# Twice the rows fetched by ScalarE, and another order for the last tiles of a graph layer

## The reference

```
h   = relu(layernorm(x))                        # x: 12500 nodes x 128
xp  = h @ lin1
C   = 0.5 * (cos(edge_weight * pi / 10) + 1)    # 212500 edges, sorted by dst
f   = softplus(edge_attr @ mlp_w1 + b1) - ln 2  # edge_attr: 212500 x 50
W   = (f @ mlp_w2 + b2) * C[:, None]
agg = segment_sum(xp[src] * W, dst)             # 12500 x 128
out = x + (softplus(agg @ lin2 + lin2_b) - ln 2) @ lin_w + lin_b
```

## Time and profile before

| what | value |
|---|---|
| median of three runs | 2056.18 us |
| the profiled execution | 2054.31 us |
| its span, first to last instruction | 2052.4 us |
| mean granted TensorE clock | 0.812 |
| TensorE busy | 1302.4 us (63%) |
| VectorE busy | 1081.9 us (53%) |
| ScalarE busy | 910.0 us (44%) |
| GpSimd busy | 1539.9 us (75%) |
| transfers, mean | 93 GB/s |

### The profile page before, as it was taken

The page is one execution under the profiler, slowest core; times in us unless marked ns, Lnnn a source line. Parts: engine busy times, 40 slices in busy tenths (PEclk is TensorE's granted clock), DMA queues, the critical chain, the costliest instruction groups (busy, mean ns, idle before and its releaser), DMA issues.

```text
span 2052.4 us, 51157 instructions
## 1 busy us (share of the span) xinstructions
PE 1302.4 (63%) x12671; PEld 1108.5 (54%) x12879; DVE 1081.9 (53%) x3364; ACT 910.0 (44%) x1536; POOL 1539.9 (75%) x1629
## 2 busy tenths in 40 slices
PE   6567666766676666656666666666656556666565
PEld 5455555555555555545555555555545445555454
DVE  8766655555555555545544445545444445454444
ACT  6664444444444444444443444434443444343442
POOL 7777777777777777777777777777777777777775
PEclk9887988888888788777887877887888788787887
DMA  9632333333333333333333333333332332333321
GB/s 319 233 88 77 85 89 78 85 90 80 90 89 79 84 88 80 91 90 80 82 90 79 90 89 79 86 85 80 89 90 71 89 89 72 89 79 82 88 72 47
DMA packets 118412, 190.46 MB, mean 93 GB/s; under 512 B 34784, under 2 KB 66000, under 8 KB 117988
## 3 DMA queue, kind: packets, MB, share of 16 engines
q0 software_dynamic: 51968, 106.53, 21.0%
q1 hardware_dynamic: 63076, 79.85, 13.2%
q10 hardware_dynamic: 3072, 0.79, 0.2%
HBM read 174.24 MB, written 12.80 MB: 91 GB/s over the span
## 4 chain that ended last, share of the span: by engine, by line
POOL 37%; issue 19%; PE 11%; SPq 10%; ACT 8%; DVE 7%; ACTq 4%; DVEq 2%; DMA 1%; POOLq 0%
POOL XG L435 37%; SPq L393 7%; ACTq L508 4%; PE PA L801 3%; PE PW L787 3%; PE PX L770 3%; SPq L389 2%; ACT TB L523 2%; ACT TB L521 2%; DVE XG L684 2%; ACT TB L519 2%; DVEq L656 1%; PE PW L784 1%; ACT XG L457 1%; DVE TB L575 1%
## 5 line engine op out<-in xcount | busy, mean ns | idle before, releaser
L435 POOL DMA_INDIRECT XG<-xp_scratch,IX x1560 | 1476.0, 946 | 475.8 <-issue 469.7
L684 DVE SCALAR_TENSOR_TENSOR XG<-PW,CC,XG 128x128 f32<-128x128 f32 x1624 | 456.8, 342 | 442.4 <-DMA XG<-xp_scratch,IX 425.7
L519 ACT ACTIVATE TB<-PX 128x512 f32<-128x512 f32 x416 | 245.7, 591 | 968.8 <-PE PX L770 477.6
L787 PE MATMUL PW<-W,TB 128*128 128x128 f32 x3322 | 538.8, 315 | 106.5 <-DVE XG L684 79.4
L787 PEld LDWEIGHTS PW<-W,TB 128*128 128x128 f32 x3322 | 535.2, 230 | 18.1
L784 PE MATMUL PW<-BPB,ones 128*128 128x512 bf16 (+1 forms) x209 | 98.9, 473 | 566.3 <-DVE XG L684 548.9
L784 PEld LDWEIGHTS PW<-BPB,ones 128*128 128x128 bf16 x416 | 40.7, 98 | 744.2 <-issue 737.1
L652 DVE SCALAR_TENSOR_TENSOR TB<-PX,TB 128x512 f32<-128x512 f32 x416 | 283.9, 682 | 274.6 <-ACT TB L523 266.8
L801 PE MATMUL PA<-OH,XG 128*64 128x64 f32 x6480 | 317.7, 271 | 0.0
L523 ACT ACTIVATE TB<-TB,HALF 128x512 f32<-128x512 f32 x416 | 299.7, 720 | 13.5
L801 PEld LDWEIGHTS PA<-OH,XG 128*64 128x64 f32 x6480 | 286.8, 182 | 32.3 <-issue 21.1
(11 more groups left out here) (86 smaller groups left out, 495.2 us busy)
## 6 DMA issues: line engine op xcount, KB each, us to landing
HT<-xp_scratch SPq DMA_DIRECT2D x3092, 0.5 KB
AT<-attr_t SPq DMA_DIRECT2D x206, 200.0 KB
XG<-xp_scratch,IX POOLq DMA_INDIRECT x1560
HA<-xp_scratch ACTq DMA_DIRECT2D x1536, 0.5 KB
AG<-zero SPq DMA_DIRECT2D x1, 6400.0 KB, 22.8
xp_scratch<-XG SPq DMA_DIRECT2D x24, 256.0 KB, 2.9
XR<-x SPq DMA_DIRECT2D x24, 256.0 KB, 5.0
out<-XR SPq DMA_DIRECT2D x24, 256.0 KB, 2.6
```

The costliest lines, as they stand in the source:

```text
L435: e.indirect_dma_start(XG[q % XG_N][0:p, k * D:(k + 1) * D], None, xp, bass.IndirectOffsetOnAxis(ap=IX[0:p, t0 + k:t0 + k + 1], axis=0)).t ...
L519: e.activation(T[:, 0:w], PX[q % X1_N][:, 0:w], ACT.Abs).then_inc(s_ab, 1)
L684: ins = e.scalar_tensor_tensor(out=G, in0=PW[q % 2][0:p, k * D:(k + 1) * D], scalar=CC[0:p, t0 + k:t0 + k + 1], in1=G, op0=ALU.mult, op1=A ...
L787: ins = e.matmul(P[0:p, k * D:(k + 1) * D], TB[q % TB_N][:, k * TILE:k * TILE + p], W2[:, :], start=False, stop=(k == n - 1), skip_group_c ...
```

## The change

- ScalarE takes 8 rows in every step from 8 on, not in every second. The first two of the rows held back go behind Abs, the next two behind Exp; then eight new numbers are loaded and the first four rows of them go behind Ln. AQ has 24 tiles, one in every 16 steps, and there are 27 buffers XG.
- The first two passes over CK go to ScalarE (`turns`), the third is done by VectorE in four parts. The conversion of the places goes to ScalarE (`places`), the base numbers also into PSUM (BQ, in PF), and the large subtraction reads them there.
- The flag is computed by ScalarE in step 18 (`far`: Abs and ReLU of the distance from the window's middle), without the product in CK, which moves to the slow path.
- The last two quads change places: quad 414 is the tile of 20 rows (fetched by SyncE), quad 415 the four full tiles. Each gather of quad 415 has a semaphore of its own, its tiles are multiplied one by one, and three of them can be scattered before the fourth is multiplied. The adds of the last two quads come one step earlier.
- Chunk 23 begins to close one step earlier. The last chunk uses PX[0] for lin2, and PX[1] and PF for lin_w; its first tile's add of x need not wait for its second.
- Quad 0's first product waits for the last ReLU (s_re) instead of the last copies (s_xe).

```diff
-    return done_by(c) + (5 if c == NNC - 1 else 6 if done_by(c) % 2 else 7)
+    return done_by(c) + (5 if c == NNC - 1 else 6 if done_by(c) % 2 or c == NNC - 2 else 7)
...
-    t0 = q * QT
+    t0 = (2 * NQ - 3 - q if q >= NQ - 2 else q) * QT
...
-HQ[NQ - 1] = len(HQ)
+HQ[NQ - 2] = len(HQ)
...
-PAIR_ROWS = 8
+TURN_ROWS = 8
 FIRST = 8
-NA = (NQ - 12 - FIRST) // 2 * PAIR_ROWS // TILE
-AQ = {FIRST + (j + 1) * TILE * 2 // PAIR_ROWS + 4: j for j in range(NA)}
+NA = (NQ - 12 - FIRST) * TURN_ROWS // TILE
+AQ = {FIRST + (j + 1) * TILE // TURN_ROWS + 4: j for j in range(NA)}
...
-    XG_N, TB_N, X1_N, OH_N = 26, 4, 4, 2
+    XG_N, TB_N, X1_N, OH_N = 27, 4, 4, 2
...
+            def turns():
+                e.wait_ge(s_tb, 16)
+                e.activation(CK[:, :], CC[:, :], ACT.Copy, scale=0.05, bias=MAGIC).then_inc(s_ck, 1)
+                e.wait_ge(s_ck, 1)
+                e.activation(CK[:, :], CK[:, :], ACT.Copy, bias=-MAGIC).then_inc(s_ck, 1)
+            def places():
+                e.wait_ge(s_dx, 16 * (11 + 2 * AT_N))
+                e.activation(BF[:, :], BI[:, :], ACT.Copy).then_inc(s_di, 1)
+                e.activation(BQ, BI[:, :], ACT.Copy).then_inc(s_di, 1)
+                e.activation(REL[:, :], DI[:, :], ACT.Copy).then_inc(s_di, 1)
+            def far():
+                e.wait_ge(s_rel, 2)
+                for p, a, b in ((TILE, 0, NT - 1), (EDGES - (NT - 1) * TILE, NT - 1, NT)):
+                    e.activation(CK[0:p, a:b], REL[0:p, a:b], ACT.Abs, bias=MID[0:p, 0:1]).then_inc(s_far, 1)
+                e.wait_ge(s_far, 2)
+                for p, a, b in ((TILE, 0, NT - 1), (EDGES - (NT - 1) * TILE, NT - 1, NT)):
+                    e.activation(VB[0:p, a:b], CK[0:p, a:b], ACT.Relu, scale=2.0, bias=MID[0:p, 1:2]).then_inc(s_vb, 1)
...
             for c in range(NPC + 3):
+                if c == NNC - 3:
+                    turns()
                 if c == NNC + 5:
                     cutoff()
+                if c == NNC + 7:
+                    places()
...
                     e.activation(T[:, 0:w], PX[q % X1_N][:, 0:w], ACT.Abs).then_inc(s_ab, 1)
+                    fetch(2)
                     e.wait_ge(s_ab, q + 1)
                     e.activation(T[:, 0:w], T[:, 0:w], ACT.Exp, scale=-1.0).then_inc(s_ex, 1)
+                    fetch(2)
                     e.wait_ge(s_ex, q + 1)
                     e.activation(T[:, 0:w], T[:, 0:w], ACT.Ln, scale=0.5, bias=HALF[:, :]).then_inc(s_ln, 1)
-                if i >= FIRST and (i - FIRST) % 2 == 0:
-                    fetch((i - FIRST) // 2 * PAIR_ROWS)
+                if i == FLAG_STEP:
+                    far()
+                if i >= FIRST:
+                    numbers((i - FIRST) * TURN_ROWS)
+                    fetch(4)
...
-            link(e.tensor_scalar(CK[:, :], CC[:, :], 0.05, MAGIC, ALU.mult, ALU.add))
-            link(e.tensor_scalar_add(CK[:, :], CK[:, :], -MAGIC))
-            e.scalar_tensor_tensor(out=CK[:, :], in0=CC[:, :], scalar=0.05, in1=CK[:, :],
-                                   op0=ALU.mult, op1=ALU.subtract).then_inc(s_cw, 1)
+            e.wait_ge(s_ck, 2)
+            for a in range(0, NT, -(-NT // 4)):
+                b = min(NT, a - (-NT // 4))
+                e.scalar_tensor_tensor(out=CK[:, a:b], in0=CC[:, a:b], scalar=0.05, in1=CK[:, a:b],
+                                       op0=ALU.mult, op1=ALU.subtract).then_inc(s_cw, 1)
...
-            link(e.tensor_tensor(rel, rel, BF[:, 0:nf].unsqueeze(2).to_broadcast([128, nf, QT]), ALU.subtract))
+            e.tensor_tensor(rel, rel, BQ[:, 0:nf].unsqueeze(2).to_broadcast([128, nf, QT]), ALU.subtract).then_inc(s_rel, 1)
...
-                pair += [i - 5] if NQ - 2 <= i - 5 < NQ else []
+                pair += [i - 4] if NQ - 2 <= i - 4 < NQ else []
...
+                        if q == NQ - 1:
+                            e.wait_ge(s_t[k], 16)
                         ins = e.scalar_tensor_tensor(out=G, in0=PW[q % 2][0:p, k * D:(k + 1) * D],
                                                      scalar=CC[0:p, t0 + k:t0 + k + 1], in1=G,
                                                      op0=ALU.mult, op1=ALU.mult)
+                        if q == NQ - 1 and k == n - 2:
+                            ins.then_inc(s_mp, 1)
...
+        def layer2(c):
+            return PX[0] if c == NNC - 1 else PF
+        def layer3(c, j=1):
+            return PX[1] if c == NNC - 1 and j == 0 else PF
...
-                    if q < X1_N:
+                    if q == 0:
                         e.wait_ge(s_re, NPC)
+                    elif q < X1_N:
                         e.wait_ge(s_xe, NPC)
...
-                    e.wait_ge(s_m, q + 1)
+                    if q < NQ - 1:
+                        e.wait_ge(s_m, q + 1)
+                    else:
+                        e.wait_ge(s_mp, 1)
...
+                        if q == NQ - 1 and k == n - 1:
+                            e.wait_ge(s_m, q + 1)
```

## The result

The changed kernel takes 2031.5 us (median of 4 runs, 2030.9 to 2033.0) against 2055.0 for the kernel before (4 runs, 2053.5 to 2058.3): ratio 0.9888, 95% interval 0.9875 to 0.99. The same kernel measured again on another chip (e10) gave 2030.92 against 2054.26: 0.9887, 0.9871 to 0.9904. It is 23.4 us faster, where 22 were predicted (2034 us). The profiled execution took 2031.51 us, span 2029.7.

What follows compares the result with a forecast made beforehand. GpSimd's gather list, then a tail, was taken to set the end. Gathers 15.0, holds 4.7 and tail 2.1 us sum to 21.8, taking 2054.3 to 2032.5 us, as a median 2034; 8-in-10 range 2026 to 2085.

Steps and rivals of the forecast that it cites:

- The gathers: GpSimd's list: 12 gathers fewer at 1.251 us each, 15.0 us less, all on the path.
- The holds: Gathers held up by VectorE's passes in the preparation and flag step: 4.7 us saved, range 3.8 to 5.8.
- the gain of the cut: Last CK pass (line 603) in four parts: 0.3 us gained, between 1.37 given back and 0.5 lost.
- The start of the steps: Preparation: work moved to ScalarE leaves the steps' start unchanged within 2 us, counted as nothing in the sum.
- ScalarE's pace: Steps with rows issued under activations: 4.07 us, 4.15 to 4.32 with closings and clamp waits, so the steps catch up.
- its limit: Slowest ScalarE step over 384 steps that still lets the steps catch up with the gathers: 4.56 us.
- rival A: ScalarE becomes the bound: each group of rows pays 0.24 us extra, time 2061 to 2126 us; chance 0.29.
- the rows run ahead of a waiting Exp: By the skill's wait queue, ScalarE would issue rows before a waiting Exp starts: step nearer 3.9 us, same end.
- Rival B: ScalarE cannot issue transfers under a running activation: some 5.9 us a step, about 2550 us; chance 0.05.
- SyncE's queue: SyncE's row transfers, 18.02 us a chunk against GpSimd's 19.3: leads the chain to about 1150 us, not the end.
- rival C: SyncE slows under twice the rows of ScalarE and sets the end, about 2052 us; chance 0.06.
- The tail: After the last gather: 1.5 us from reordered last quads, 0.6 from the last chunk's own banks, 2.1 us in all.

Runs made afterwards that it cites:

- e10: The changed kernel itself, unaltered, measured again on another chip: 2030.92 us against 2054.26 for the kernel before, ratio 0.9887.
- e1: Changed kernel with ScalarE fetching 12 tiles again, eight rows every second step, and GpSimd 12 gathers more: 2048.79 us, ratio 0.9968.
- e8: Changed kernel with VectorE's passes put back: whole CK passes, casts and place subtraction from SBUF, flag at step 18: 2038.94 us, ratio 0.9921.
- e4: Changed kernel with the last pass over CK in one piece instead of four: 2032.69 us, ratio 0.9895.
- e7: e6 with a 25th tile fetched by ScalarE, its rows issued in steps 392 to 407: 2030.69 us, ratio 0.9886.
- e2: Changed kernel with ScalarE's eight rows placed 0, 4, 4 behind Abs, Exp and logarithm instead of 2, 2, 4: 2128.1 us.
- e3: Changed kernel with all eight of ScalarE's rows behind the logarithm, none behind Abs or Exp: 2331.4 us.
- e6: Changed kernel with VectorE's step 418 multiplying quad 415 before the adds of quads 412 to 414: 2031.54 us, ratio 0.9889.
- e9: Changed kernel with the old tail: old quad order, products together, last chunk in PF, chunk 23 a step later: 2034.99 us, ratio 0.9899.

## Why the prediction was right

The sum was 21.8 us; the span of the profiled execution fell by 22.7, the median by 23.4. By its terms:

- **The gathers, 15.0 us: right.** 12 x 1.251, and in e1 16.2, of which 1.2 are slightly longer gathers.
- **The holds, 4.7 us: mis-sized.** 20.8 us ahead of the tail less 15.0 leaves 5.8, and e8 loses 6.4 when all of them come back. Two sizes were off: I took the gain of the cut at 0.3 us, and it was 1.37 - 0.41 = 1.0 in the profiled execution (0.6 to 1.2 by the other traces); and I left out two gathers of 1.15 and 1.25 us, 0.5 us over 0.94:
```profile
68.40 1.15 POOL L420 DMA_INDIRECT XG<-x,IX  x1 [0.30 <-issue]
...
116.17 1.25 POOL L435 DMA_INDIRECT XG<-xp_scratch,IX  x1 [0.30 <-issue]
```
  The upper end of my range for this term, 5.8, was the value. The Trainium skill (SBUF — State Buffer, on ports) has it that the lock is held for the whole instruction. The trace agrees: uncut, the held gather ends 0.81 us after the pass (before, e8, e4), and in four pieces it gets in earlier, for 0.27 + 0.14 us of hold beside 1.04 in one.
- **The start of the steps, "unchanged within 2 us": wrong by 1, at no cost.** The first attribute load of the steps moved from 124.45 to 127.58 us, 3.1 us later. In e8, without ScalarE's added passes, it is at 123.67, and in the other traces with them between 125.83 and 130.67. The steps caught up all the same. The cost that I did not count is at GpSimd: a late start eats the margin of the 27th buffer, as e7 shows (0.56 us).
- **ScalarE's pace: right in its mechanism, just above its range.** 0.77 + 0.77 + 2.64 = 4.18 us against 0.76 + 0.76 + 2.55 = 4.07, and 4.35 with closings and clamp waits against 4.15 to 4.32. This was the step that decided, and its limit was looser than I said (by the estimate of e2 and e3 4.65 instead of 4.56): the prices of rival A, 2061 to 2126, were some 36 us too high, and its chance of 0.29 rested on that limit. Its mechanism, a surcharge of 0.24 us in each group, does not exist under activations. Nor did the rows run ahead of a waiting Exp, which would have made the step 3.9 us: those behind Exp start 0.14 us after its own start.
- **Rival B** (no issue under an activation) is refuted by the same rows.
- **SyncE's queue, and rival C: right, and refuted.** Its chunks take 17.33 us before ScalarE's rows begin and 17.83 us with twice as many of them (below), as in the earlier trace rows; it leads the chain from 600 to about 1200 us (forecast: to about 1150). The adds after 1000 us, forecast at 83 or 84, were 86 for the same reason.
- **The tail, 2.1 us: right as a sum (2.0), wrong in its parts, and partly luck.** The last chunk's product starts at E + 5.6 instead of the forecast E + 4.8 (before: E + 6.3): 0.7 us instead of 1.5. The scatter of 412 and 413, which I timed at E - 0.6, came at E + 0.45, at half clock (0.50, 1.2 GHz) and 1.98 us long. Behind the product 1.2 us were won instead of 0.6; 0.46 of it is the product itself, 0.62 us instead of 1.08, and that is the granted clock (1.00 instead of 0.50), luck of this execution. I counted the earlier close of chunk 23 as hidden beside gather waits. It was not: the chain of waits runs through its matmuls (L882 and L883) until 2013.22 us, and through the products of quads 414 and 415 behind them on TensorE, to the scatter.

SyncE's timeline after, attribute loads, which begin its chunks.
```profile
127.58 0.69 SPq L352 DMA_DIRECT2D AT<-attr_t  x2
144.91 0.70 SPq L352 DMA_DIRECT2D AT<-attr_t  x2
162.74 0.73 SPq L352 DMA_DIRECT2D AT<-attr_t  x2
```

## What to carry to other kernels

Where one engine's list is the bound, count its instructions first, and then ask of every other engine only how late it may be at which point; a slack of this kind must be counted up to where the late engine's work changes (here the last 24 steps, 2.9 instead of 4.5 us each). In this kernel, issue work on a busy engine's queue was nearly free where it was dealt out in portions as long as the activation ahead of it, and dear when it was put in one place: 4.35, 4.93 and 5.46 us a step for the same eight transfers. At the very end, before a late transfer is put down to a neighbour, look whether the traces in which it came in time have the same neighbour.

## What was not expected of the hardware

- The first row transfer behind a register load takes ScalarE 0.45 us, the first one under an activation 0.21 us, though both follow an interruption.
- The last gather of 128 rows landed 2.4 to 2.7 us after its start in nine traces, and after 3.4, 3.4 and 4.4 us in three (e6, e7, e8), where one of its 16 parts came late. A 256 KB store close ahead of it is not enough for that: the changed kernel has it too and lands in 2.5 us.
- The last gather of a list of the same length ended up to 1.9 us apart between executions (2016.56, 2016.90, 2017.76 and 2018.44 us, in e10, the changed kernel, e6 and e9), and the same tail took 12.3 to 13.5 us: differences of that size between single traces are no effect.
